# LayerNorm statistics in a two-stage attention kernel: twelve one-column VectorE operations written as four over 128x4

## The reference

```
def _layernorm(x, axis=-1, eps=1e-05):
    m = jnp.mean(x, axis=axis, keepdims=True)
    v = jnp.var(x, axis=axis, keepdims=True)
    return (x - m) / jnp.sqrt(v + eps)

x = x + tanh(g_xattn) * xattn(_layernorm(x), ctx, ...)   # 8 heads of 64, keys and values from ctx (1024 x 384)
x = x + tanh(g_ffn)   * ffn(_layernorm(x), ...)          # 16 heads of 32, q normalised per head, gated output
```

## Time and profile before

| | |
|---|---|
| median of 3 runs | 5059.6 us (5053.59 to 5064.68) |
| profiled execution, its own time | 5053.59 us |
| its span, first to last instruction | 5051.8 us |
| mean granted TensorE clock | 0.977 of 2.4 GHz |
| TensorE matmuls busy | 4766.1 us (94%), 21696 instructions |
| VectorE busy | 2946.6 us (58%), 4019 instructions |
| ScalarE busy | 2601.4 us (51%), 4705 instructions |
| GpSimd busy | 3367.3 us (67%), 2667 instructions |

### The profile page before, as it was taken

One profiled execution on the slowest core, in us unless ns is written; L12 is line 12 of the kernel. 1 busy time (PEld: TensorE's weight loads), 2 busy tenths in 40 slices (PEclk: granted clock), 3 DMA queues, 4 the chain that ended last, 5 costly groups with the idle time before them and its releaser, 6 DMA issues.

```text
span 5051.8 us, 67410 instructions
## 1 busy us (share of the span) xinstructions
PE 4766.1 (94%) x21696; PEld 2731.3 (54%) x21696; DVE 2946.6 (58%) x4019; ACT 2601.4 (51%) x4705; POOL 3367.3 (67%) x2667
## 2 busy tenths in 40 slices
PE   4999999999999999998998999999999999999997
PEld 3555555556565556564564554554654644645644
DVE  4454545454545454566766656757656666666563
ACT  2444445353535354536636646546556556466454
POOL 1656656574756565747848858767578588578587
PEclk7999999999999999999999999999999999999998
DMA  7343535344343434333233132322323322332320
GB/s 239 97 130 113 129 112 125 117 123 125 97 134 88 142 88 133 93 88 86 57 100 76 45 110 64 84 84 63 94 70 76 93 62 64 92 82 53 101 51 26
DMA packets 285210, 481.11 MB, mean 95 GB/s; under 512 B 32832, under 2 KB 165440, under 8 KB 275648
## 3 DMA queue, kind: packets, MB, share of 16 engines
q1 hardware_dynamic: 284864, 476.79, 34.6%
HBM read 223.14 MB, written 50.33 MB: 54 GB/s over the span
## 4 chain that ended last, share of the span: by engine, by line
PE 50%; DVE 5%; issue 3%; ACT 2%; POOL 1%; SPq 1%; DMA 0%; ACTq 0%; POOLq 0%; DVEq 0%
PE aux L839 15%; PE acc L942 10%; PE aux L902 10%; PE scores L925 9%; DVE nm L1286 4%; PE aux L954 2%; PE aux L963 1%; PE aux L883 1%; POOL added_f L817 1%; PE aux L859 1%; SPq L734 1%; ACT probs L1128 1%; DMA stack<-ck_lo 0%; PE aux L911 0%; DVE st L1223 0%
## 5 line engine op out<-in xcount | busy, mean ns | idle before, releaser
L1286 DVE TENSOR_REDUCE nm<-aux 128x1 f32<-128x1024 f32 x1536 | 1844.7, 1221 | 1192.8 <-PE aux L902 1190.0
L817 POOL TENSOR_TENSOR added<-added,probs 128x512 f32<-128x512 f32 x1433 | 1804.4, 1297 | 856.7 <-PE acc L942 653.4
L1128 ACT ACTIVATE probs<-scores 128x512 f32<-128x512 f32 x2151 | 1189.1, 597 | 862.5 <-PE scores L925 831.3
L925 PE MATMUL scores<-stack 128*128 128x512 f32 x4096 | 1340.3, 417 | 36.3 <-ACT probs L1128 15.8
L902 PE MATMUL aux<-stack 96*128 96x512 f32 (+1 forms) x3072 | 1017.5, 420 | 94.1 <-DVE nm L1286 53.6
L925 PEld LDWEIGHTS scores<-stack 128*128 128x128 f32 x4096 | 735.3, 190 | 639.2 <-ACT probs L1128 223.7
L942 PE MATMUL acc<-probs,vh 128*32 128x512 f32 (+1 forms) x4302 | 968.8, 617 | 20.0 <-ACT vh L1095 20.0
L902 PEld LDWEIGHTS aux<-stack 96*128 96x128 f32 (+1 forms) x3072 | 525.6, 190 | 578.1 <-DVE nm L1286 272.1
L817 POOL TENSOR_TENSOR added_f<-added_f,probs 128x512 f32<-128x512 f32 x537 | 678.9, 1298 | 59.1 <-PE acc L942 36.9
L839 PE MATMUL aux<-xT_hi,wqk 128*128 128x512 f32 x1536 | 580.2, 407 | 13.7 <-ACT qwork L1067 6.9
L1128 ACT ACTIVATE more<-scores 128x512 f32<-128x512 f32 x537 | 300.3, 598 | 155.6 <-PE scores L925 134.7
(11 more groups left out here) (131 smaller groups left out, 4938.1 us busy)
## 6 DMA issues: line engine op xcount, KB each, us to landing
wqk<-w_split SPq DMA_DIRECT2D x256, 256.0 KB, 3.8
wvo<-w_split SPq DMA_DIRECT2D x64, 1024.0 KB, 6.9
stack<-cq_hi SPq DMA_DIRECT2D x128, 256.0 KB, 5.0
stack<-ck_hi SPq DMA_DIRECT2D x128, 256.0 KB, 4.9
stack<-cq_hi SPq DMA_DIRECT2D x256, 128.0 KB, 2.3
stack<-ck_hi SPq DMA_DIRECT2D x256, 128.0 KB, 2.4
xs<-in_x SPq DMA_DIRECT2D x16, 1024.0 KB, 6.4
stack<-cq_lo SPq DMA_DIRECT2D x64, 256.0 KB, 4.9
```

Source lines behind the costliest of these rows:

```text
L817: pool.tensor_tensor(onto, onto, exp_buffer(T, e), ALU.add).then_inc(added_ok, 1)
L925: ins = pe.matmul(scores[:, u % SCORES, :], stack[:, g % 2, e * ph.SLOTS + ks, jt * P:(jt + 1) * P], stack[:, g % 2, e * ph.SLOTS + qs, n ...
L1128: act.activation(exp_buffer(T, e), scores[:, (n - 1) % SCORES, :], ACT.Exp, scale=ph.SCALE).then_inc(probs_ok, 1)
L1286: dve.tensor_reduce(nm[:, e * TT + t:e * TT + t + 1], keys, axis=AX.X, op=ALU.max, negate=True).then_inc(emptied["dve"], 1)
```

## The change

`mv` loses its EPS column, `rs` its fourth row. L1228 becomes one scalar_tensor_tensor over 128x4, max(variance + EPS, variance), with `mv` as both tensor inputs. ScalarE's Copy goes. The three groups of four column operations become four linked operations over 128x4: y*y, (y*y * -0.5) * (variance + EPS), (that + 1.5) * y, and (-mean) * y. Each has two tensor inputs in SBUF (`mv` and `rs` are SBUF tensors).

```
-        mv = sb("mv", [P, TT, 3])
-        rs = sb("rs", [P, 4, TT])
+        mv = sb("mv", [P, TT, 2])
+        rs = sb("rs", [P, 3, TT])
...
                         link(act.activation(rs[:, 1, r], rs[:, 0, r], ACT.Ln))
-                        link(act.activation(rs[:, 1, r], rs[:, 1, r], ACT.Exp, scale=-0.5))
-                        act.activation(rs[:, 3, r], rs[:, 1, r], ACT.Copy, scale=-0.5).then_inc(rstd_ok, 1)
+                        act.activation(rs[:, 1, r], rs[:, 1, r], ACT.Exp, scale=-0.5).then_inc(rstd_ok, 1)
...
-                dve.memset(mv[:, :, 2], EPS)
+                def newton(y, x, y2, out):
+                    link(dve.scalar_tensor_tensor(y2, y2, -0.5, x, ALU.mult, ALU.mult))
+                    return dve.scalar_tensor_tensor(out, y2, 1.5, y, ALU.add, ALU.mult)
...
-                            dve.tensor_reduce(rs[:, 0, r], mv[:, r, 1:3], axis=AX.X, op=ALU.add).then_inc(rstd_in, 1)
+                            dve.scalar_tensor_tensor(rs[:, 0, r], mv[:, r, 1], EPS, mv[:, r, 1], ALU.add, ALU.max).then_inc(rstd_in, 1)
...
-                        column = lambda i, t: rs[:, i, t:t + 1]
-                        tiles = range(r.start, r.stop)
-                        for t in tiles:
-                            ins = dve.tensor_scalar(column(2, t), column(1, t), column(1, t), column(0, t), ALU.mult, ALU.mult)
-                        link(ins)
-                        for t in tiles:
-                            ins = dve.tensor_scalar(column(1, t), column(2, t), 3.0, column(3, t), ALU.subtract, ALU.mult)
-                        link(ins)
-                        for t in tiles:
-                            ins = dve.tensor_scalar(column(0, t), mv[:, t, 0:1], column(1, t), -1.0, ALU.mult, ALU.mult)
-                        ins.then_inc(norm_in, 1)
+                        link(dve.tensor_tensor(rs[:, 2, r], rs[:, 1, r], rs[:, 1, r], ALU.mult))
+                        link(newton(rs[:, 1, r], rs[:, 0, r], rs[:, 2, r], rs[:, 1, r]))
+                        dve.scalar_tensor_tensor(rs[:, 0, r], mv[:, r, 0], -1.0, rs[:, 1, r], ALU.mult, ALU.mult).then_inc(norm_in, 1)
```

More of the change, by code:

```diff
@@ L1225, in _ @@
                             for t in tiles:
-                                ins = dve.bn_aggr(mv[:, r.start + t, 0:2], st[:, r.start + t, :])
+                                ins = dve.bn_aggr(mv[:, r.start + t, :], st[:, r.start + t, :])
                             link(ins)
-                            dve.tensor_reduce(rs[:, 0, r], mv[:, r, 1:3], axis=AX.X, op=ALU.add).then_inc(rstd_in, 1)
+                            dve.scalar_tensor_tensor(rs[:, 0, r], mv[:, r, 1], EPS, mv[:, r, 1], ALU.add, ALU.max).then_inc(rstd_in, 1)
                             continue
```

## The result

The changed kernel takes 5174.3 us, median of four runs (5155.7 to 5205.7), against 5056.9 (5053.6 to 5064.7) for the kernel before on the same chip: ratio 1.0238, 95% interval 1.0207 to 1.0268. It is slower by 117 us, where 96 was forecast. The profiled execution took 5195.9 (span 5194.1), 142 above that of before.

The account below looks back on a forecast made before the run. TensorE works 94% of the span, so only what makes it wait was taken to count. Longer chains 77 us, clock 20, start -1 summed to +96, forecast 5155 us, range 5068 to 5230 (8 in 10).

Parts of the forecast that it names:

- rival A: Nothing excludes at 128x4, so the change gains what its instruction count says: -20 us, 5040; chance 0.12.
- B: VectorE waits once for GpSimd, then keeps its turn through its linked operations: 5060, no change; chance 0.06.
- attention first halves: Seven half batches where TensorE waits 1.84 and 1.77 us: chains mean 3.3 us longer, 23 us in all.
- The forecast's mechanism: VectorE operations with two SBUF inputs and GpSimd's adds exclude each other for the whole instruction, also at 128x4; chance 0.62.
- one add for each operation, in all three kinds: In 22 of 32 half batches each block operation waits for one GpSimd add: block 5.3 us for 2.03, chain +3.7.
- FFN second halves: Seven half batches where TensorE stands 4.55 us for the scaling: chains mean 3.6 us longer, 25 us in all.
- attention second halves: Eight half batches with no named wait for the chain: +4.0 less 0.4 slack, 3.6 us each, 29 in all.
- priced at +0.4: The L1228 replacement waits 0.62 us on average, takes 0.06 longer, and the dropped ScalarE step returns 0.24.
- rival C: VectorE is kept out to the end of GpSimd's run, twice per chain: 128 us, with the clock 145, about 5205; chance 0.13.
- the two statistics reductions: FFN second halves: L1286 reductions (2.34 us) queued behind the L1228 replacement, late by its 1.0 us wait, delaying TensorE's transposes.
- The clock: TensorE's granted clock falls after longer stands: 14 us in attention second halves, 7 in first halves, together 20 (bounds 0 and 40).
- The signs that were to tell the cases apart: Block medians near 1.4 us, transposes' wait 4.55 to about 8, new 3.6 us attention-product waits, mean clock below 0.977.

Follow-up runs that it names:

- e1_sum_only: The kernel before with only the reduction L1228 replaced by the change's 128x4 operation with two SBUF inputs: 5152.4 us, ratio 1.0201.
- e7_link_each_eighth: The changed kernel with each eighth GpSimd add waiting for the add before it: 5104.4 us; the kernel before with the same links: 5043.8 us.
- e3_sum_one_input: The kernel before with the reduction L1228 replaced by a 128x4 tensor_scalar with one SBUF input: 5161.8 us, ratio 1.0209.
- e5_reductions: The kernel before with the chain as short as in the change, but built of five reductions and two ScalarE steps: 5043.1 us, ratio 0.9950.

## Why the prediction was right, and where it was wrong

- *The direction and the sum.* 5155 was forecast, 5174 came, inside the range. That VectorE's new operations and GpSimd's adds exclude each other also at 128x4 was right (L1231's 1.2 us median against 0.16 for the free one), and so rival A was out; B was out by the four operations of attention first halves, each of which waits for an add of its own. That the sum came so near is in part luck. The forecast's mechanism alone costs 53 to 61 us and not 96, and what was too much there made up for most of what the kept-out operations added.
- *The step that failed: one add for each operation, in all three kinds.* It held for attention first halves (forecast 23 us, measured 18). In FFN second halves 25 was forecast and 48 measured, in attention second halves 29 and 38. There it was not the block: it took 0.73 in the first and 1.75 in the second, because L1231, priced at +0.4, had already sat out the row. I had taken 34 waits of L1302 for one add against two long ones as odds that hold anywhere. They depend on the place: of the 34 short ones 28 came after five unbroken adds or fewer, the other six after 16 or 17 and the two long ones after 13 and 17, that is most of them 11 or 12 adds after another VectorE turn. In the runs with the change or a part of it, the exposed operations that came first in a second half had 10 to 19 adds behind them. Half of rival C came true, in L1231's place. e1_sum_only shows that this one operation is enough, e7_link_each_eighth what the forecast's own mechanism costs by itself: 53 to 61, with 96 forecast.
- *What stood behind L1231.* I had named the two statistics reductions queued behind it, and priced them at 1 us. The larger damage went through ScalarE: its logarithm waits, the exponentials stand behind it, and TensorE loses 8.24 us before a score product.
- *Reasons given for the exclusion.* "All five read two tensors in SBUF" was true and not the whole of it: e3_sum_one_input loses as much with one tensor. The old column operations were safe for their width, not for their single tensor.
- *Sizes.* A free scalar_tensor_tensor in SBUF takes 0.16, not the 0.22 of L1337, whose inputs are partly in PSUM: the free block is 0.73 to 0.76, not 0.94. The clock took 29.5 us of TensorE's busy time, with 20 forecast (bounds 0 and 40). The chains of the start are 3 us shorter, with 1 forecast. The L1297 kept out, some 20 us of the profiled difference, had no term.
- *The signs that were to tell the cases apart.* Of them only the new waits at the attention products (4.8 us for some 3.6), L1231's median and the lower clock (0.965) came. The block's medians are 0.16 us, which the list would have read as rival A, and single operations above 6 us in 14 of 22 chains, which it would have read as rival C. The transposes' wait fell from 4.55 to 3.15, because the long wait came earlier, at the score products.
- *Rival A's price.* It said that the shorter chain would be worth 20 us if nothing excluded it. e5_reductions is close to that case: 26 us below the kernel before beside it.

## What to carry to other kernels

Before an edit makes VectorE operations fewer, look at what GpSimd does at that place and at the kind of each new operation: reductions, one-column tensor_scalars and operations with an input in PSUM passed beside GpSimd's adds here, four-column tensor_scalars in SBUF and all with two SBUF inputs had to wait. Then look at who stands behind the one that waits, for a 0.16 us instruction with two engines queued behind it cost 2% of this kernel. Long unbroken rows of GpSimd work are worth breaking: a link on each eighth add cost nothing (ratio 0.9978), the long waits were gone, and the ten runs lay within 11 us.

## What the runs showed of the hardware that I had not expected

- A VectorE operation that waits for GpSimd is not always let in at the next instruction boundary. After up to 10 back-to-back adds it was (1.02 us at most for a 0.16 us operation), after 15 it was kept out until the row ended (5.89 us with five adds left), at 12 it went either way, and with a 0.08 us gap between the adds never.
- With such gaps two linked operations get in for one add: 1.13, 0.16, 1.11, 0.16 us, where without gaps each of the four waits for its own.
- A tensor_scalar of 128x4 takes 0.17 to 8.6 us in the place where four of 128x1 take 0.144 each and never wait.
